# An ALiBi attention stage as a straight program of 64 (kv head, query tile) steps, with one 512-column mix for four heads

## What is computed

```python
q = (x @ Wq.T).reshape(b, s, H, HD)      # H = 32, HD = 128, s = 1024, x is 1024 x 512
k = (x @ Wk.T).reshape(b, s, HKV, HD)    # HKV = 8: four query heads share one kv head
v = (x @ Wv.T).reshape(b, s, HKV, HD)
q = _rmsnorm(q, q_norm_w); k = _rmsnorm(k, k_norm_w)
scores = einsum('bkgqd,bksd->bkgqs', q, k) / sqrt(HD)
bias = where(rel > 0, NEG_INF, slopes * rel)          # rel = key position - query position
attn = softmax(scores + bias)
out = einsum('bkgqs,bksd->bkgqd', attn, v)
x = x + out.reshape(b, s, H * HD) @ Wo.T
```

## Time and profile before

| | |
|---|---|
| median of 3 runs | 1810.41 us (1809.52 to 1810.6) |
| span of the profiled execution | 1807.0 us, 3.4 us under that median |
| ALiBi stage, first matmul (584.24) to last add | 584.2 to 1742.7 us |
| busy share of the span | PE 89%, PEld 71%, DVE 62%, ACT 45%, POOL 25% |
| mean granted TensorE clock | 0.949 of 2.4 GHz |
| L1393, add with division, 128x512 | 256 of 750 ns |

### The profile page before, as it was taken

The page is one execution under the profiler, slowest core; times in us unless marked ns, Lnnn a source line. Parts: engine busy times, 40 slices in busy tenths (PEclk is TensorE's granted clock), DMA queues, the critical chain, the costliest instruction groups (busy, mean ns, idle before and its releaser), DMA issues. The chain is left out here.

```text
span 1807.0 us, 32358 instructions
## 1 busy us (share of the span) xinstructions
PE 1601.9 (89%) x10264; PEld 1275.3 (71%) x10264; DVE 1129.4 (62%) x2719; ACT 815.2 (45%) x2197; POOL 449.9 (25%) x686
## 2 busy tenths in 40 slices
PE   3966699799986899989989989989989998999979
PEld 2742344344575788878878869878878887887867
DVE  5437577577656367466566556657656747657675
ACT  2540455455421364356257246337336535625611
POOL 3003000000102243234125116115224413513320
PEclk9985899899987999989999999999999999999989
DMA  3135442244101010010001001001001100100011
GB/s 133 36 108 103 70 49 37 37 57 52 49 7 47 1 39 22 1 32 30 1 15 48 1 8 42 13 3 48 13 2 31 30 1 23 39 1 13 1 42 48
DMA packets 39252, 60.14 MB, mean 33 GB/s; under 512 B 5878, under 2 KB 18422, under 8 KB 39030
## 3 DMA queue, kind: packets, MB, share of 16 engines
q1 hardware_dynamic: 39054, 57.65, 14.1%
HBM read 49.03 MB, written 9.96 MB: 33 GB/s over the span
## 5 line engine op out<-in xcount | busy, mean ns | idle before, releaser
L1449 DVE CUSTOM_DVE_ANT_0 ab_prob<-ps,ab_bias 128x128 f32<-128x128 f32 (+7 forms) x256 | 192.8, 753 | 152.6 <-issue 147.0
L713 DVE TENSOR_REDUCE ra_part_max<-ps 128x1 f32<-128x512 f32 (+1 forms) x450 | 219.5, 548 | 91.4 <-PE ps L603 47.2
L1354 ACT CAST ab_pt_h<-ps 128x512 fp32r<-128x512 f32 (+3 forms) x384 | 171.6, 482 | 180.6 <-PE ps L1246 180.3
L1461 DVE TENSOR_TENSOR ab_pt_l<-ps,ab_pt_h 128x512 fp32r<-128x512 f32 (+3 forms) x384 | 201.8, 553 | 28.8 <-ACT ab_pt_h L1354 24.4
L1359 ACT ACTIVATE ab_prob<-ab_prob,ab_neg_max 128x128 f32<-128x128 f32 (+7 forms) x256 | 199.9, 781 | 43.6 <-DVE ab_neg_max L1449 37.9
L72 PE MATMUL ps<-ab_pt_h,ab_v_h 128*128 128x256 f32 x640 | 201.2, 314 | 12.4 <-ACT ab_o_raw L1366 12.4
L701 ACT ACTIVATE ra_pt<-ps 128x1024 f32<-128x1024 f32 x128 | 130.1, 1023 | 174.5 <-PE ps L633 132.1
L1393 DVE SCALAR_TENSOR_TENSOR x<-ps,ab_recip,x 128x512 f32<-128x512 f32 x256 | 180.1, 750 | 31.7 <-PE ps L74 30.7
L1327 ACT ACTIVATE ab_squares<-ps 128x128 bf16<-128x128 f32 x320 | 83.7, 281 | 237.6 <-PE ps L74 237.6
L72 PE MATMUL ps<-b_w_h,b_xt_h 128*128 128x512 f32 (+1 forms) x512 | 177.9, 347 | 2.2 <-DVE ab_pt_l L1377 2.2
L74 PE MATMUL ps<-ab_pt_h,ab_v_l 128*128 128x256 f32 x640 | 179.8, 281 | 0.0
(11 more groups left out here) (182 smaller groups left out, 3598.1 us busy)
## 6 DMA issues: line engine op xcount, KB each, us to landing
ab_raw<-in_wqkv SPq DMA_DIRECT2D x28, 384.0 KB, 3.0
ab_raw<-in_wbo SPq DMA_DIRECT2D x32, 256.0 KB, 2.7
ra_q_st<-parts SPq DMA_DIRECT2D x54, 128.0 KB, 6.2
ra_k_st<-parts SPq DMA_DIRECT2D x54, 128.0 KB, 6.7
parts<-pa_stage SPq DMA_DIRECT2D x24, 256.0 KB, 3.3
a_raw<-in_wa SPq DMA_DIRECT2D x4, 768.0 KB, 9.7
f_raw<-in_wf SPq DMA_DIRECT2D x8, 324.0 KB, 4.0
x<-in_x SPq DMA_DIRECT2D x8, 256.0 KB, 5.6
```

The source lines that it names most:

```text
L713: dve.tensor_reduce(part_max[:, c, u:u + 1], ps[:, banks[n % len(banks)], 0:k1 - k0], AX.X, ALU.max).then_inc(piece_max, 1)
L1354: act.copy(pt_h[:, job % 2, s0:s0 + nb, col:col + P], ps[:, 4 + n % 3, 0:nb * P].rearrange("p (j q) -> p j q", q=P)).then_inc(pt_high, 1)
L1449: dve.tensor_tensor_reduce(out=prob[:, s % 3, 0:w], in0=ps[:, 2 * (s % 2):2 * (s % 2) + 2, :].rearrange("p a b -> p (a b)")[:, 0:w], in1=b ...
L1461: dve.tensor_tensor(pt_l[:, job % 2, s0:s0 + nb, col:col + P], ps[:, 4 + n % 3, 0:nb * P].rearrange("p (j q) -> p j q", q=P), pt_h[:, job ...
```

## The change

The loop over kv heads and its two phases go. The stage is written out in 64 steps t, one for each kv head t // 8 and query tile i = t % 8, with two steps ahead of them and two behind. A step has 8 slots s. In step t, TensorE scores tile t (one bank of at most 512 columns in a slot, one or two per head), turns the weights of tile t - 1 from slot 2 on (one key block of all four heads at a time, into one bank) and mixes them with v two slots later, 512 columns wide, projects q, k and v of tile t + 2 in slots 0 to 3, turns q and k of tile t + 1 in slot 0, and makes the output projection of tile t - 2 in slot 6, with the four heads summed in its bank. Banks 0 and 1 hold scores, 2 and 3 the projection (one set instead of two), 4 to 6 are a ring for q, k, weights and outputs, and 7 is the mix. The weights are now divided by their row sums on GpSimd before they are turned (`normalise`), the slope is a constant of the score instruction (no bias tile), and the high halves of the weight matrices go from GpSimd to ScalarE.

```diff
+def turned_in(t, s):
+    u, j = (t - 1, s - 2) if s >= 2 else (t - 2, s + B_SLOTS - 2)
+    return (u, j) if 0 <= u < B_STEPS and j <= u % NT else None
+def mixed_in(t, s):
+    u, j = (t - 1, s - 4) if s >= 4 else (t - 2, s + B_SLOTS - 4)
+    return (u, j) if 0 <= u < B_STEPS and j <= u % NT else None
...
 GpSimd:
-            powers(0)
-            with pool.Fori(0, KVB - 1) as g:
-                split_step(g, False)
-                powers(g + 1)
-            split_step(KVB - 1, True)
+            def normalise(t, h):
+                w = P * (t % NT + 1)
+                pool.wait_ge(recip_done, GB * t + h + 1)
+                pool.tensor_scalar(prob[:, t % 2, h, 0:w], prob[:, t % 2, h, 0:w], recip[:, t % 2, h:h + 1], None,
+                                   ALU.mult).then_inc(normed, 1)
...
 TensorE:
+            def turn_qk(t):
+                pe.wait_ge(scaled, t + 1)
+                ring_free("q", t)
...
+            def mix(u, j):
+                i, n = u % NT, blocks_before(u) + j
+                if j == 0 and u:
+                    pe.wait_ge(o_out, u)
+                pe.wait_ge(emptied, job_of["p", u, j] + 1)
+                at = (u - i + j) % VR
+                three_pass(pe, ps[:, 7, :], (v_h[:, at, :], v_l[:, at, :]),
+                           (pt_h[:, n % PT, :], pt_l[:, n % PT, :]), j == 0, j == i).then_inc(mixed, 1)
+            def project_out(u):
+                pe.wait_ge(o_low, u + 1)
+                if u % NT == 0:
+                    pe.wait_ge(split, 2 * KC * (u // NT) + KC)
+                ring_free("o", u)
+                for h in range(GB):
+                    last = three_pass(pe, ring_bank("o", u), (o_h[:, h * P:(h + 1) * P], o_l[:, h * P:(h + 1) * P]),
+                                      (wo_h[:, h, :], wo_l[:, h, :]), h == 0, h == GB - 1)
...
+            for t in range(-2, B_STEPS + 2):
+                for s in range(B_SLOTS):
+                    if 0 <= t < B_STEPS and score_piece(t % NT, s):
+                        score(t, *score_piece(t % NT, s), n)
+                        n += 1
+                    if s == 0 and 0 <= t + 1 < B_STEPS:
+                        turn_qk(t + 1)
+                    if turned_in(t, s):
+                        turn(*turned_in(t, s))
+                    if s < KC and 0 <= t + 2 < B_STEPS:
+                        project(t + 2, s)
+                    if mixed_in(t, s):
+                        mix(*mixed_in(t, s))
+                    if s == 6 and 0 <= t - 2 < B_STEPS:
+                        project_out(t - 2)
...
 VectorE, in the same loop over t and s:
+                    if 0 <= t < B_STEPS and score_piece(t % NT, s):
+                        shift(t, *score_piece(t % NT, s), n)
+                        n += 1
...
+                    if turned_in(t, s):
+                        pt_low_of(*turned_in(t, s))
+                    if s in (2, 4, 6) and 0 <= t < B_STEPS:
+                        invert(t, s // 2 - 1)
...
+                    if s == 6 and 0 <= t - 2 < B_STEPS:
+                        u = t - 2
+                        dve.wait_ge(out_done, u + 1)
...
+                        dve.tensor_tensor(x[:, u % NT, :], ring_bank("o", u), x[:, u % NT, :], ALU.add).then_inc(emptied, 1)
+                    if s == 7 and 0 <= t + 2 < B_STEPS:
+                        scale_qk(t + 2)
```

More of the change, by code:

```diff
@@ L1059, in alibi_attention_block @@
[L1059 to L1062, removed]
+        qt_h = sb("qt_h", [P, 2, GB, P], F32R)
+        qt_l = sb("qt_l", [P, 2, GB, P], F32R)
+        kt_h = sb("kt_h", [P, PAD + 2 * T], F32R)
+        kt_l = sb("kt_l", [P, PAD + 2 * T], F32R)
+        v_h = sb("v_h", [P, VR, DB], F32R)
+        v_l = sb("v_l", [P, VR, DB], F32R)
+        nat = sb("nat", [P, GB + 1, DB])
@@ L1144, in _ @@
+            for g in range(KVB):
+                for k in range(KC):
+                    load(2 * KC * g + k, g, k, True)
+                for k in range(KC):
+                    if g + 1 < KVB:
+                        load(2 * KC * g + KC + k, g + 1, k, False)
         @block.gpsimd
         def _(pool):
[L1146 to L1186, removed]
@@ L1194, in _ @@
         @block.tensor
         def _(pe):
[L1196 to L1204, removed]
-                cols = slice(i * P, (i + 1) * P)
[L1206 to L1211, removed]
-                last.then_inc(projected, 1)
@@ L1239, in turn @@
-            def turn(g, v):
-                pe.wait_ge(exped, 1 + U * g + v + 1)
-                for k, (j0, nb) in enumerate(key_groups(v % NT)):
-                    n = groups_before_b(v) + k
-                    if n >= 3:
-                        pe.wait_ge(pt_low, 1 + NG * g + n - 2)
-                    for j in range(nb):
-                        last = pe.transpose(ps[:, 4 + n % 3, j * P:(j + 1) * P],
-                                            prob[:, v % 3, (j0 + j) * P:(j0 + j + 1) * P], const["ident"][:, :])
-                    last.then_inc(turned, 1)
@@ L1250, in mix @@
-            def mix(g, job, part):
-                pair = job % 4
-                if part == 0:
-                    pe.wait_ge(pt_low, 1 + NG * g + groups_before_b(2 * job + 2))
-                    if job == 0:
-                        pe.wait_ge(added, 1 + NO * g)
-                    else:
-                        pe.wait_ge(o_out, 1 + JOBS * g + job)
-                for j in range(part * (pair + 1), (part + 1) * (pair + 1)):
-                    at = place(pair, j)
-                    last = three_pass(pe, ps[:, 7, 0:PAIR], (v_h[:, j, :], v_l[:, j, :]),
-                                      (pt_h[:, job % 2, at, :], pt_l[:, job % 2, at, :]),
-                                      j == 0, j == 2 * pair + 1)
-                if part == 1:
-                    last.then_inc(mixed, 1)
@@ new lines, in turn @@
+            def turn(u, j):
+                if j == 0:
+                    pe.wait_ge(normed, GB * (u + 1))
+                ring_free("p", u, j)
+                for h in range(GB):
+                    last = pe.transpose(ring_bank("p", u, j)[:, h * P:(h + 1) * P], prob[:, u % 2, h, j * P:(j + 1) * P],
+                                        const["ident"][:, :])
+                last.then_inc(turned, 1)
+            def mix(u, j):
[6 more added lines that the diff above has]
+                           (pt_h[:, n % PT, :], pt_l[:, n % PT, :]), j == 0, j == i).then_inc(mixed, 1)
@@ L1469, in _ @@
[L1469 to L1477 removed]
+            dve.memset(slope_sq[:, :, GB:GB + 1], 1.0 / DB).then_inc(made, 1)
+            slopes = const["slopes"][:, :].rearrange("p (g h) -> p g h", h=GB)
```

522 lines of the change are left out of this document (249 added, 273 removed).

## The result

The changed kernel takes 1983.2 us (median of 4 runs, 1979.1 to 1989.9); the kernel before took 1810.0 beside it. The ratio is 1.096, 95% interval 1.094 to 1.099. The forecast was 1860 us, with a range from 1815 to 1915: the direction was right, the size was not. The profiled execution spans 1980.9 us.

A forecast was written before the change was run, and what follows sets the result against it. TensorE bounds the ALiBi stage (89% work, 11% stops). A kv head becomes 126.6 + 10.4 + 9.8 + 0.8 = 147.6 us (147.4 by steps); with start and tail the stage takes 1208 against 1158.5, giving 1860 us, range 1815 to 1915.

The forecast's parts named there:

- Mixing: Weights times v on TensorE: 36 blocks x 3 matmuls, 24.8 us instead of 28.1, minus 3.3 per kv head.
- The old stops: TensorE's waits in the old loop (loop's head, output eviction, adds, row maxima), 12.7 us a kv head, expected to go.
- the low clock: Old kernel, after the loop's head: TensorE at 1.2 GHz loses 3.5 us a kv head, expected to go.
- The work left: A kv head of the changed ALiBi stage if no new waits came: 126.6 us.
- The first chain: Output projection (slot 6) waits for GpSimd's low output half, behind head 1's division: 10.4 us of stops a kv head.
- the price N of the division: GpSimd's division within the first chain, priced like a cast: 0.3 us at 128 columns to 1.05 at 1024.
- the rival at the subtraction's rate: GpSimd's division runs at the two-input rate, 1.32 ns a column more, 49 us in all: 1909 us; chance 0.14.
- The second chain: Turn of next q and k (slot 0) waits for VectorE's scaling behind the add: 9.8 us, plus 0.8 restarts, a kv head.
- The clock: Rival: TensorE's clock falls in every kv head, at tile i = 2, 3.5 us each, 28 in all: 1888 us; chance 0.12.
- Start and tail: ALiBi stage's ends: 47 us for the two steps ahead and steps 0 and 1, 19 for the last two steps.
- neither chain would be covered: Forecast that both new TensorE waits show; rival with one covered 1776 us, both 1692; chance of one or both 0.14.

The follow-up runs named there:

- Run 8: Changed kernel with the division moved from GpSimd to ScalarE, one exponential late, and VectorE scaling q and k ahead of the finished tile's add: 1723.1 us (0.953 of before).
- run 6: Changed kernel with 12 more 256-column TensorE matmuls ahead of each output projection's wait for the low half of the output: 1944.4 us (1.075 of before).
- run 1: Changed kernel with GpSimd's division working on one column instead of 128 to 1024, waits and signals kept: 1831.3 us (1.012 of before).
- run 2: Changed kernel with GpSimd's two output halves (cast and subtraction) issued ahead of the division of head 1 in slot 4: 1845.6 us (1.019 of before).
- run 10: Changed kernel with the division moved from GpSimd to ScalarE, one exponential late, VectorE's order unchanged: 1797.6 us (0.994 of before).
- Run 3: Changed kernel with VectorE scaling q and k in slot 6, ahead of the finished tile's add, instead of slot 7: 1906.6 us (1.053 of before).
- run 7: Changed kernel with the division moved from GpSimd to VectorE, right behind each reciprocal: 1814.4 us (1.003 of before).
- run 4: Changed kernel with VectorE's five-column `ms_eps` made by the kernel before's instruction, one tensor input instead of two: 1982.0 us, against 1983.2.

## Why the prediction was wrong in size

**The terms that went.** Mixing was to give 3.3 us, and the columns fell by 3.2. The old stops were put at 12.7 us and the low clock at 3.5. In the account they are 8.2 and 2.6. For the stops I had summed the rows of the weight loads, and a weight load starts to wait while matmuls ahead of it still run. For the clock I had read the one stretch of a single round. That 12.7 + 3.5 filled the 16 us that were missing was chance: by the account stops and low clock are 10.8 us, and what remains lies in the changeovers and restarts, which I had priced too low, and in the length of that one round.

**The work left**, 126.6 us. Run 8 has almost no stops and shows 121.9 + 6.6, less 3 restarts of 0.26, so about 127.8: 1.2 more. The 0.26 us of a restart is an estimate, the difference of the rests, (10.5 - 6.6) us, over 17.8 - 3.0 stops. Rows of run 6 give nearly the same: behind the stop at 1018.77 the second matmul starts 0.34 us after the first instead of 0.23, and a stop is printed from the end of the matmul before, 0.40 us behind its start, where the next could have started after 0.23; 0.11 + 0.17 = 0.28 us.

**The first chain** is the step that failed, by the size of one term. The mechanism and the place were right (runs 1, 2 and 10 each take most or all of its wait away), the price N of the division was not. I took 0.3 to 1.05 us for it, from the cast; it is 0.61 to 2.85. Over the eight steps that is 8.5 us more, and with it the 10.4 would have been 18.9; measured are 15.7 of stops, with 8 restarts 17.8. By tile, i = 0 to 7, TensorE stopped 0.8, 1.9, 3.5, 2.3, 1.8, 1.7, 1.8 and 2.0 us, where 0.9, 2.3, 2.5, 1.7, 1.0, 0.8, 0.65 and 0.55 were forecast: for the narrow divisions of i = 0 and 1 nothing is missing, for the widest 1.4 us. The price was taken from the row that looked nearest, and even the bound was none: the rival at the subtraction's rate, 1.32 ns a column more than the cast, means 2.15 ns, and the division takes 2.5. The same term put GpSimd at 59 us a kv head; it was busy 91.

**The second chain** was forecast at 9.8 us and 0.8 of restarts; 8.1 and 2.1 are measured. Run 3 confirms the mechanism. That the two sums, 10.6 and 10.2, lie so near is in part luck, since the stops were put 1.7 too high and the restarts 1.3 too low.

**The clock.** The prediction gave one stretch of 3.5 us a kv head as a rival, and put the low clock at nothing in the forecast. There are 3 to 5, of 1.3 to 2.7 us each, 5.8 us in all: this term is the second part of the miss. From rows that showed the low clock behind a stop of 3.0 us and not behind one of 0.98 I took it for rare; behind stops of 1.8 us it comes too, though not behind each (21 stretches, 35 such stops). Run 6 shows the cause: with the idling filled, the stretches go.

**What was not named** is 0.9 us at the turn for the division of head 3, and 0.3 for `o_raw`, together 1.7 with their restarts.

The sum of these differences is 1.2 + 7.4 - 0.4 + 5.8 + 1.7 = 15.7 us a kv head, where 162.9 - 147.4 = 15.5 were missed. **Start and tail** need no term of their own: the periods make 124 us, and 123 were missed.

**The rivals** were laid out as if only one could hold. The dear division and the falling clock held together, and the first brought the second about through its stops: without the long division there is no low clock (run 1). 1860 + 49 + 28 = 1937 would have been the sum of the two, still 46 short. That neither chain would be covered was right; that a division on another engine covers the first one, and turns +9.6% into -0.6% (run 10), was not seen.

It stays open why GpSimd's divisions let `ms_eps` pass in the changed kernel and, in the form of run 4, hold it at some widths only, and what all the holds together cost the changed kernel.

## What to carry to other kernels

An operation whose price no row shows needs bounds that are real: if none of the engine's rows has its form, the upper bound is open, and if it stands once in each step on the chain that the tensor engine waits for, that opening, times the number of steps, is the width of the range. Ask of an off-path engine not how busy it is but what stands ahead of the one instruction that others wait for: GpSimd was 40% busy, yet two of its instructions moved ahead of one brought 138 us. Many stops of about 2 us cost more than their length: here some 0.26 us for each restart, and 5.8 us of low clock a kv head.

## What the runs showed of the hardware

- GpSimd multiplies a tile by a value per partition at 0.29 us + 2.5 ns a column (2847 ns at 1024), in fp32 from and to SBUF. At 1024 columns VectorE does it in 0.75 us (run 7, where GpSimd doesn't hold it) and ScalarE in 1.16 (run 8).
- VectorE and GpSimd can hold each other until the end of an instruction in SBUF: 2.24 us for a division that takes 0.62 (run 7), 1.25 for five columns that take 0.15 (the changed kernel). In the changed kernel GpSimd's casts and subtractions did this to the five columns, its divisions did not.
- In the changed kernel TensorE's clock fell to 1.2 GHz during or after stops of 1.8 to 3.5 us, 21 times in six kv heads; 1.4 us of matmuls ahead of each wait for `o_l` reduced the 21 stretches to 3 (run 6).
- By the estimate above, a stop costs TensorE about 0.26 us beside what is printed for it.
